# Attention over a graph's edges: source rows gathered once per unit into a ring and copied to the pairs, small loads moved to ScalarE's queue

## The reference

```
h_l, h_r = x @ weight_l, x @ weight_r
e     = sum(leaky_relu(h_l[dst] + h_r[src], 0.2) * att, -1)      # per edge and head
alpha = exp(e - segment_max(e, dst)[dst]) / segment_sum(...)[dst]
out   = segment_sum(h_r[src] * alpha, dst) + bias
```

## Time and profile before

| | |
|---|---|
| median of the runs | 3260.66 us |
| the profiled execution's own time | 3259.94 us |
| its span | 3258.2 us |
| mean granted TensorE clock | 0.974 |
| TensorE busy with matmuls | 3095.0 us (95%) |
| GpSimd busy | 928.0 us (28%) |
| ScalarE busy | 1397.0 us (43%) |
| VectorE busy | 1335.6 us (41%) |

### The profile page before, as it was taken

How to read it: one execution, slowest core, us unless ns; L and a number is a source line. 1 busy time by engine, 2 the same in 40 slices (tenths; PEclk the granted TensorE clock), 3 DMA queues, 4 the chain that set the end, 5 groups by cost and what they waited for, 6 DMA issues and landing times. The chain is left out here.

```text
span 3258.2 us, 45328 instructions
## 1 busy us (share of the span) xinstructions
PE 3095.0 (95%) x14598; PEld 2017.7 (62%) x14598; DVE 1335.6 (41%) x3056; ACT 1397.0 (43%) x2510; POOL 928.0 (28%) x1063
## 2 busy tenths in 40 slices
PE   7979999979999997999999999999999999999998
PEld 6865555558888885777777555555555555555554
DVE  7960111126666667999999411111111111111112
ACT  6950001235555555888778423333332222223233
POOL 4530000047777763777777200000000000000000
PEclk9989999989999988999999999999999999999999
DMA  2666667623333323776666566666666677777774
GB/s 83 262 241 265 267 276 289 271 58 83 88 83 83 83 66 93 191 195 184 184 185 181 232 283 283 283 283 283 283 283 283 283 292 292 293 292 293 292 298 164
DMA packets 165548, 709.30 MB, mean 218 GB/s; under 512 B 38135, under 2 KB 131938, under 8 KB 152271
## 3 DMA queue, kind: packets, MB, share of 16 engines
q1 hardware_dynamic: 126713, 618.83, 49.4%
q0 software_dynamic: 33600, 83.09, 9.4%
q10 hardware_dynamic: 5011, 4.48, 0.5%
HBM read 657.91 MB, written 48.07 MB: 217 GB/s over the span
## 5 line engine op out<-in xcount | busy, mean ns | idle before, releaser
L1448 PE MATMUL deep_out_psum<-deep_adjacency,deep_scaled_nodes_odd 125*128 125x450 f32 (+1 forms) x1750 | 669.7, 538 | 0.0
L1448 PE MATMUL deep_out_psum<-deep_adjacency,deep_scaled_nodes 125*128 125x450 f32 (+1 forms) x1750 | 669.7, 538 | 0.0
L1696 POOL DMA_INDIRECT source_rows<-gat_source_rows,pair_src x416 | 396.1, 952 | 575.3 <-POOLq L64 448.8
L1448 PEld LDWEIGHTS deep_out_psum<-deep_adjacency,deep_scaled_nodes_odd 125*128 125x128 f32 x1750 | 329.2, 190 | 299.0 <-issue 298.2
L1448 PEld LDWEIGHTS deep_out_psum<-deep_adjacency,deep_scaled_nodes 125*128 125x128 f32 x1750 | 328.9, 190 | 298.1 <-issue 297.3
L2136 POOL DMA_INDIRECT near_room<-gate_source_rows,pair_src x416 | 396.6, 953 | 141.7 <-issue 121.3
L1506 ACT ACTIVATE deep_squares_high<-deep_aggregate,deep_vectors 128x450 fp32r<-128x450 f32 (+1 forms) x70 | 46.8, 668 | 618.1 <-DVE deep_aggregate L1578 618.1
L1448 PE MATMUL gcn_out_psum<-adjacency_columns,gcn_scaled_nodes 125*128 125x450 f32 (+1 forms) x700 | 269.0, 539 | 0.0
L2241 PE MATMUL gate_banks<-edge_weights,edge_features_t 128*128 128x256 f32 x832 | 248.5, 380 | 0.0
L1448 PEld LDWEIGHTS gcn_out_psum<-adjacency_columns,gcn_scaled_nodes 125*128 125x128 f32 x700 | 131.6, 190 | 123.4 <-issue 122.8
L1592 DVE SCALAR_TENSOR_TENSOR deep_normed<-deep_aggregate,deep_vectors,deep_squares 128x450 f32<-128x450 f32 (+1 forms) x70 | 47.9, 684 | 384.9 <-ACT deep_squares L1515 384.9
(11 more groups left out here) (423 smaller groups left out, 4902.1 us busy)
## 6 DMA issues: line engine op xcount, KB each, us to landing
deep_adjacency<-adjacency SPq DMA_DIRECT2D x69, 5625.0 KB, 16.3
adjacency_columns<-adjacency SPq DMA_DIRECT2D x19, 5625.0 KB, 16.3
adjacency<-adjacency_columns SPq DMA_DIRECT2D x7, 5625.0 KB, 17.7
edge_features<-in_edge_attr_dram SPq DMA_DIRECT2D x416, 64.0 KB
att_node_rows<-pair_dst_rows SPq DMA_DIRECT2D x104, 128.0 KB, 3.3
gate_node_rows<-pair_dst_rows SPq DMA_DIRECT2D x104, 128.0 KB
source_rows<-gat_source_rows,pair_src POOLq DMA_INDIRECT x416, 2.7
near_room<-gate_source_rows,pair_src POOLq DMA_INDIRECT x416, 2.8
```

What stands on the lines that cost most here:

```text
L1448: m = nc.tensor.matmul(op[:, n % 2, 0:cols], h[l % 2][:, s, :], ring[0:T, n % 2, s, 0:cols], start=s == 0, stop=s == NS - 1)
L1696: pool.indirect_dma_start(xj[:, b % HOLD, q, :], None, d["h_r"], bass.IndirectOffsetOnAxis(ap=c["pair_src"][:, b * PQ + q:b * PQ + q + 1], ...
```

## The change

Three things change in the attention.

1. **The gather.** GpSimd no longer gathers for each pair but once for each unit (392 gathers, 391 units and one more) into a new ring `held` of 48 places. It waits before each gather for the landing of the gather 6 before it, and every 4th time for the copies that free ring places. Each gather also counts up `s_gi` when it has been issued, which tells that the one 6 before has landed. SP now fills `xj` from the ring, with one copy inside SBUF of 64 KB for each of the 416 pairs. It reads the ring place of each pair and the count to wait for from a table (`pair_words`). `HOLD` goes from 14 to 11.
2. **The small loads.** Node rows and breaks move from SP's queue to ScalarE's. In its iteration `i` ScalarE issues, between `sloped(i-1)` and `copy_ends`, the node rows of block i+3, and where i mod 4 = 2 the 4 transfers of breaks as well.
3. **The tables.** In the first convolution stage TensorE makes 4 more transposes, VectorE counts the ring places in some twelve operations on one partition (`turns`), and ScalarE stores `pair_src` to memory, from where the gated layer's own copy is loaded with the bridge's weights.

The core of the diff:

```
 class EdgePath
     def stores(self, act, n):
         if n == 9:
+            act.wait_ge(self.s_dl, 2)
+            act.dma_start(self.d["pair_src"], self.pair_src[:, :]).then_inc(self.s_st, 16)
...
     def tensor(self, pe, n):
         if n == 9:
...
+            for t in range(UTL):
+                nc.tensor.transpose(ps[:, 0, t * 128:(t + 1) * 128], self.src_f[:, t, :], c["ident"][:, :])
...
     def vector(self, dve, n):
+        if 5 <= n < 5 + TURNS:
+            k = n - 4
+            if k == 1:
+                vec.tensor_scalar(self.turns[:, :], c["pair_edge"][:, :], 128.0 * UNITS_HELD, None, ALU.is_ge).then_inc(self.s_tn, 1)
...
-HOLD = BEHIND + 6
+HOLD = BEHIND + 3
...
         def _(pool):
-            for b in range(NPB):
-                if b >= HOLD:
-                    pool.wait_ge(s_msg, b - HOLD + 1)
-                for q in range(PQ):
-                    pool.indirect_dma_start(xj[:, b % HOLD, q, :], None, d["h_r"],
-                                            bass.IndirectOffsetOnAxis(ap=c["pair_src"][:, b * PQ + q:b * PQ + q + 1], axis=0)).then_inc(s_g[b % HOLD], 16)
...
+            for u in range(UNITS_GATHERED):
+                if u >= LANDED_BEHIND:
+                    landed(u - LANDED_BEHIND)
+                done = (u + PQ - UNITS_HELD + NS - 1) // PQ - 1
+                if u % PQ == 0 and done >= 0:
+                    pool.wait_ge(s_cp[done % HOLD], 16 * PQ * (done // HOLD + 1))
+                pool.indirect_dma_start(held[:, u % UNITS_HELD, :], None, d["h_r"], bass.IndirectOffsetOnAxis(ap=c["unit_src"][:, u:u + 1], axis=0),
+                                        engine_sem=s_gi).then_inc(s_g[u % len(s_g)], 16)
...
         def _(sp):
+            def copies(b):
+                slot = four(nc, sp, c["pair_words"][32:33, :], b, UNITS_HELD - 1)
+                last = sp.value_load(c["pair_words"][64:65, b * PQ + PQ - 1:b * PQ + PQ], min_val=1, max_val=UNITS_GATHERED + LANDED_BEHIND)
+                if b >= HOLD:
+                    sp.wait_ge(s_msg, b - HOLD + 1)
+                sp.wait_ge(s_gi, last)
+                for q in range(PQ):
+                    sp.dma_start(xj[:, b % HOLD, q, :], held[:, bass.ds(slot[q], 1), :].rearrange("e o f -> e (o f)")).then_inc(s_cp[b % HOLD], 16)
...
         def _(act):
+            def node_rows(b):
+                if b >= 4:
+                    act.wait_ge(s_oht, b - 3)
+                act.dma_start(dr[:, b % 4, :], d["pair_dst"][b * PQ:(b + 1) * PQ, :].rearrange("k e -> (k e)").unsqueeze(0).to_broadcast([128, L])
+                              ).then_inc(s_dr[b % 4], 16)
+
+            def load_breaks(s):
+                if s >= 3:
+                    act.wait_ge(s_d, s - 2)
+                for h in range(HEADS):
+                    act.dma_start(breaks[h * SB:(h + 1) * SB, s % 3, :, :], d["breaks"][:, s * SB:(s + 1) * SB, :].rearrange("w j e -> j w e")
+                                  ).then_inc(s_bk[s % 3], 16)
+            for b in range(3):
+                node_rows(b)
...
                 if 1 <= i <= NPB:
                     sloped(i - 1)
+                if i + 3 < NPB:
+                    node_rows(i + 3)
+                if i % PER_SB == 2 and i < NPB:
+                    load_breaks(i // PER_SB)
                 if at(i, 2) is not None:
                     copy_ends(at(i, 2))
```

More of the change, by code:

```diff
@@ L712 @@
 OUTSIDE = 4000
+UNITS_HELD = 48
+UNITS_GATHERED = NU + 1
+LANDED_BEHIND = 6
+TURNS = (UNITS_GATHERED - 1) // UNITS_HELD
 class EdgePath:
@@ L730, in __init__ @@
         self.passed = room[0:NS - 1, NS * D + 2 * KP:NS * D + 3 * KP]
+        self.turns = room[0:1, NS * D + 2 * KP:NS * D + 3 * KP]
+        self.pair_src = self.unit.bitcast(I32)
         self.work = sb("path_work", [128, 16 * 128])
@@ L889, in vector @@
             vec.tensor_copy(c["lane_passes"][0:1, :, :].rearrange("o w (a k) -> o w a k", a=4), turned[0:1, :, :, 0:KC])
+        if n == 13:
+            vec.tensor_scalar(c["pair_words"][64:65, :], c["pair_edge"][:, :], 1.0 / 128, 1.0 + LANDED_BEHIND, ALU.mult, ALU.add)
+        if 5 <= n < 5 + TURNS:
+            k = n - 4
+            if k == 1:
+                vec.tensor_scalar(self.turns[:, :], c["pair_edge"][:, :], 128.0 * UNITS_HELD, None, ALU.is_ge).then_inc(self.s_tn, 1)
+            else:
+                dve.wait_ge(self.s_tn, k - 1)
+                vec.scalar_tensor_tensor(self.turns[:, :], c["pair_edge"][:, :], 128.0 * k * UNITS_HELD, self.turns[:, :], ALU.is_ge, ALU.add).then_inc(self.s_tn, 1)
+        if n == 5 + TURNS:
+            dve.wait_ge(self.s_tn, TURNS)
+            vec.tensor_scalar(self.turns[:, :], self.turns[:, :], -128.0 * UNITS_HELD, None, ALU.mult).then_inc(self.s_tn, 1)
+            dve.wait_ge(self.s_tn, TURNS + 1)
+            vec.tensor_tensor(self.turns[:, :], c["pair_edge"][:, :], self.turns[:, :], ALU.add).then_inc(self.s_tn, 1)
+            dve.wait_ge(self.s_tn, TURNS + 2)
+            vec.tensor_scalar(c["pair_words"][32:33, :], self.turns[:, :], 1.0 / 128, None, ALU.mult)
 SPANS = [(k, min(BW, N - k)) for k in range(0, N, BW)]
@@ L1639, in attention @@
         passes = sb("lane_passes", [1, NSB, 2, HEADS, SB + 1], BF16)
+        held = sb("unit_rows", [128, UNITS_HELD, D])
         xj = sb("source_rows", [128, HOLD, PQ, D])
@@ L1675, in attention @@
          s_fl, s_dp, s_c, s_cc, s_hf, s_tp, s_d, s_k, s_kk, s_sl, s_x, s_w, s_wc, s_msg, s_A, s_rs, s_O, s_hv) = (c["sems"].take("att_" + n) for n in names)
-        s_g = [c["sems"].take(f"att_sources_gathered_{k}") for k in range(HOLD)]
+        s_gi = c["sems"].take("att_gathers_issued")
+        s_g = [c["sems"].take(f"att_unit_gathered_{k}") for k in range(LANDED_BEHIND + 2)]
+        s_cp = [c["sems"].take(f"att_sources_copied_{k}") for k in range(HOLD)]
         s_dr = [c["sems"].take(f"att_node_rows_loaded_{k}") for k in range(4)]
@@ L1709, in _ @@
             for b in range(NPB):
-                k, s = b % 4, b // PER_SB
                 if b == BRIDGE_AT:
                     meanwhile(sp)
[L1713 to L1722, removed]
+                copies(b)
             for b in range(NPB - 4, NPB):
@@ L1730, in terms @@
             def terms(b):
[L1731 removed]
+                tile = four(nc, pe, c["pair_words"][0:1, :], b, NS - 1)
                 pe.wait_ge(s_oht, b + 1)
[L1733 removed]
+                pe.wait_ge(s_cp[b % HOLD], 16 * PQ * (b // HOLD + 1))
                 if b >= 2:
@@ L1981, in merge @@
             def merge(b):
-                tile = four(nc, dve, c["pair_tile"], b, NS - 1)
+                tile = four(nc, dve, c["pair_words"][0:1, :], b, NS - 1)
                 s = b // PER_SB
@@ L2229, in core @@
             def core(b):
-                tile = four(nc, pe, c["pair_tile"], b, NS - 1)
+                tile = four(nc, pe, c["pair_words"][0:1, :], b, NS - 1)
                 pe.wait_ge(s_et, b + 1)
```

35 lines of the change are left out of this document (22 added, 13 removed).

## The result

The changed kernel takes 3360.89 us (median of 4 runs, 3355.66 to 3372.5), the kernel before, beside it on the same chip, 3261.47 us (4 runs, 3260.34 to 3263.78). The ratio is 1.0312, with a 95% interval of 1.0296 to 1.0327. The change makes the kernel slower by 3.1%; the prediction was 3352 us, in a range of 3285 to 3395.

A forecast was written before the change was run, and what follows sets the result against it. GpSimd's gathers and TensorE with the maximum's chain, close together, were taken to bound the attention. 24 superblocks (+80.0), start (+9.2), first delayed chain (+1.4) and tables (+0.5) gave +91.1 us: 3352 us, range 3285 to 3395.

The forecast's parts named there:

- The late chain: Attention: five issues ahead of `copy_ends` delay the scan, exponents and TensorE's turn by 1.4 us a superblock.
- upper bound of 2.7 us: Attention: largest delay of the maximum's chain per superblock, if each issue on ScalarE took 0.7 us.
- The clock: Attention: TensorE's longer pauses bring one fall of the clock in every superblock, costing 3.5 us each.
- No hold: Rival: ScalarE's five issues run beside its other work in the attention; faster, middle 3247 us; chance 0.17.
- SP too slow: Rival: copies hold the blocks if SP takes over 5 us for one, estimate 2.9; chance 0.05 with anything else.
- The gather: Attention: 24 fewer gathers, GpSimd needs 18.83 us a superblock and stops being the limit where TensorE takes more.
- The start: Ahead of the first terms: block 0 waits for 10 gathers, copies and a landing, +9.2 us.
- Part 3: First convolution stage: four more transposes on TensorE add 0.5 us, VectorE's twelve operations hide under matmuls.
- the sum: Whole kernel: all terms together add 91.1 us to the profiled execution's 3259.94 us.
- all falls long: Upper case of the forecast's own range, 3305 to 3385 us: attention superblocks of 24.4 us, +100 + 11 us.
- A sign read wrongly: Attention: the exponents' wait for VectorE was to grow from 2.2 us to above 3.5 us.

The follow-up runs named there:

- loads alone: The kernel before with only node rows and breaks issued by ScalarE at the changed kernel's places, gathers per pair as before: 3345.62 us, ratio 1.0264.
- filler experiment: The changed kernel with six more filler matmuls on TensorE just ahead of the turn of the weights, once per superblock: 3286.72 us, ratio 1.0081.
- first experiment: The changed kernel with the four break transfers issued behind `onehots` where i mod 4 = 0, not ahead of `copy_ends`: 3268.98 us, ratio 1.0021.

## Why the prediction was right

**The late chain.** Right in place and mechanism. Shown by moving the breaks alone (loss nearly gone), by adding the loads alone (+85 us), and by the rows: over the 24 superblocks `copy_ends` now starts on average 2.9 us after `sloped` instead of 0.6, the scan 3.25 instead of 1.27. The term was too small, 1.4 us: the turn is 8.23 us after `sloped` instead of 6.25, 2.0 us more. The step that was off is mainly the price of an issue. It was taken from SP's queue, 1.85 us for four. On ScalarE's 14 of the 26 groups of four took 1.8 to 2.0 us as well, but the others up to 3.27, with one issue in the four, not always the first, of up to 1.55 us; the mean is 2.28. The single issues (duration ns min/median/max):

```profile
L1867 ACTq DMA_DIRECT2D lane_breaks<-segment_break_rows x104: 326/450/1552, 717.8 to 1314.4; - x104
```

With the loads alone the mean of four is 2.02 us and the delay 1.6, so the ring and its copies beside them account for a part of it. Another 0.1 us is the step from the last issue to the first copy, which the prediction left out. The upper bound of 2.7 us held.

**The clock.** Right: a fall in each superblock, at a price of 24.15 - 18.65 - 2.0 = 3.5 us, the 3.5 predicted; the filler experiment gives 3.67 by its profile and 3.1 by the medians. That the number fits so well is partly luck. The prediction took two falls of 10.2 us to one of 3.4; there were 16 of 10.2, one of 13.7 and seven of 6.8, and none of 3.4. So the falls were longer than taken, and a microsecond of them cost less than the 4.35 / 10.2 taken from the kernel before. The Trainium skill (TensorE: Matmul & The Clock Gate, "HAM oscillation — how this bites in real kernels") describes a loop whose regular pause brings the lower clock back in each turn. The trace agrees, with 24 falls in 24 superblocks and 3 once the pause was filled. The pauses are short here: TensorE's longest idle time between two matmuls in the 24 superblocks is 1.6 us, and 0.8 us in the kernel before.

**The rivals.** "No hold" was wrong: the engine's next instruction starts 0.1 us behind its queue's last issue. The Trainium skill (DMA: Bandwidth & Descriptors, "Issuing engines are not separate DMA queues") says that starting transfers from several engines saves only the time to initiate them, usually small beside the transfer. The trace has that time at 2.28 us for four loads, and it decided here by its place, since it held a step on which VectorE and TensorE wait. "SP too slow" was wrong too: TensorE waited for copies in 2 places, 18.4 us, nearly all of it the start. But it was nearer than the prediction had it. A copy's issue takes 0.509 us in the median, 2.0 us a block; with the register loads in front, of 0.82 and 0.44 us, a block takes SP some 4.1 us and not the estimated 2.9. That is 16.5 us a superblock, 2 us below the 18.65, and with the small loads on SP as well it was too much, as the experiment with part 2 undone shows. The tile of copies in the changed kernel (duration ns min/median/max):

```profile
L1751 SPq DMA_DIRECT2D source_rows<-unit_rows x416: 485/509/1800, 704.7 to 1303.3; - x139
```

**The gather.** Right that it stops being the limit, and that this is worth nothing as long as a superblock takes over 20.2 us. What I hadn't foreseen is what comes then: with the chain back in place (first experiment) it is still worth only 2.1 us over 24 superblocks, since short falls took the rest.

**The start.** Right: 9.3 us against 9.2, and 14.3 with seven gathers against 18.0 with ten: (18.0 - 14.3) / 3 = 1.23 us for each gather less, one step of the gather.

**Part 3 and the rest.** Mis-sized or open. The first gather came 3.8 us later, not 0.5. Across the kernels it starts at 687.2 (before), 688.3 (loads alone, without part 3), and with part 3 at 688.9 to 691.0. So part 3 costs some 1 to 3 us, and what of it is its own isn't settled. The 3.2 us behind the superblocks were not predicted; the other traces of the change have 2041.4 to 2043.3 there against 2041.6, so at most 1.7 us of them are seen elsewhere, and the rest is open. Against the span the sum was 91.1 and the difference 112.6 us; against the medians it is 99.4, because the profiled execution stood 11.6 us above its median. One of the prediction's own sums does not come out: with all falls long it has +100 + 11, which is 3372 us, and not the 3385 given as the upper end.

**A sign read wrongly.** I had said that the exponents' wait for VectorE would grow above 3.5 us. It is 44.3 / 24 = 1.85 us, below the 2.17 of the earlier trace rows. ScalarE was late itself, so its `onehots` and `share` fell into that wait, and its new idle time stands in front of `copy_ends` instead, as a wait for nothing but issue.

## What to carry to other kernels

Here a DMA issue on ScalarE's queue held all that stood behind it there. Before such loads are moved to a compute engine, look for the step in that engine's loop on which other engines wait, and put the issues behind it, where the engine idles anyway: here the same four transfers cost some 90 us more in one place than in another. When a limit is lifted, ask what the freed engine will run into: here it was the clock, and filling TensorE's pause was worth more than the removed gathers.

## What the runs showed of the hardware

- The clock's falls can recur with a loop. At a superblock of 20.2 us, paced by gathers, there were 10 falls in 24; no longer paced by them, with the same chain, 19; with the chain 2 us late, 24. Six filler matmuls in the pause brought that to 3.
- On ScalarE's queue an issue of node rows took 0.34 us in the median; one of the four break transfers 0.45 us in the median and up to 1.55.
- A copy inside SBUF with its place from a register takes the issuing queue 0.51 us in the median; with the register loads, four take some 4.1 us, so the copies of four blocks fill 16.5 us of SP's time.
- Waiting for a gather three back, some 3.7 us at 1.249 us each, is not free beside copies: 68 waits, 41.5 us. With six back no such wait stood in the changed kernel's trace.
- On two chips the same kernel took 3731.8 and 3805.67 us instead of 3260, with ScalarE standing still again and again. There neither the size nor the sign of a difference of ten us could be told.
